# Second feed-forward of a two-stage block in fp32: order of GpSimd's subtractions, place of the sums' split, waits per bank, and x folded by two additions

## The chip, the core and the metric

The kernel runs on one core of a Trainium2 chip. The metric is the device time in microseconds (us) of one execution. A core has TensorE (matrix multiplications into eight PSUM banks of 128 x 512 fp32), VectorE, ScalarE, GpSimd, and SyncE, which here only issues transfers. Each engine works through its own list of instructions in order, and the engines wait for each other by semaphores. In the profile they are PE (PEld is TensorE's loading of weights), DVE, ACT, POOL and SP.

## The reference

The input is x, 2048 rows of 1024. Two stages follow each other, each with a residual addition and a normalisation over the row:

```
s  = silu(x @ w_gate.T);  s[the half of each row with the smallest |s|] = 0
x1 = layernorm(x + (s * (x @ w_up.T)) @ w_down.T)           # 2752 hidden

lin(x, wq, A, B) = x @ tile(wq, (1, 4)).T + 0.5 * (x @ A.T @ B.T)   # rank 2
y  = layernorm(x1 + lin(silu(lin(x1, w1q, a1, b1)) * lin(x1, w3q, a3, b3), w2q, a2, b2))
```

In the second stage each weight is stored for a quarter of its input width and repeated four times. So x1 may first be folded: its four quarters of 256 columns are added, and the product has a depth of 256 instead of 1024. The same holds for the hidden values, 2752 folded to 688. The low-rank parts use the unfolded values.

## The kernel before

The 2048 rows are four blocks of 512 (`NB`), each four tiles of 128 (`NT`). Products keep fp32 precision by splitting each operand into a high part of the type fp32r and a low part, the rest; `three` (L1357 to L1359) multiplies high by high, high by low and low by high. ScalarE rounds to the high part, GpSimd subtracts to get the low part of weights.

The first stage (gate, up and down products and the search for the median) is not touched. The second stage begins near 1494 us and has these parts:

1. Opening. For each of the eight tiles of blocks 0 and 1 TensorE transposes x1 (`turn_x`, L1511), ScalarE copies the result out of PSUM into one of two buffers `x1T` (L856), TensorE multiplies it by A (`low_rank`, L1528), and VectorE folds it into `xf` (`fold_x`, L1225), rounds (`xsh`) and subtracts (`xsl`). ScalarE may overwrite a buffer when `l_fold` says that the fold two tiles before has read it. After four tiles `low_rank_x` (L1238 to L1241) prepares `lx`, the low-rank part, for TensorE.
2. A pass over the weights, `pairs(0)`, for blocks 0 and 1 (`bb` 0 and 1): 11 steps `p`, each with two blocks. For one step and one block TensorE fills four banks (gate and up of two pieces `i`; the banks alternate between 0 to 3 and 4 to 7), 48 matmuls and 4 small ones (L1566). ScalarE makes `sg` = silu of the gate banks (L879). VectorE multiplies by the up banks (`h`, L1253), adds into `fold` (L1258 to L1262) and accumulates two low-rank sums in `acc` (L1273). After each second step, and after the last, a piece of the folded hidden values is complete: ScalarE rounds it (`hq0h` or `hq1h`, L862) and GpSimd subtracts (`hq0l`, `hq1l`; `low_q`, L628). The weights of a step, w1 and w3, come by two transfers; ScalarE rounds (`w13h`, L846), GpSimd subtracts (`w13l`; `low_13`, through the helper L533). They have two buffers; the transfer for step p + 2 waits until TensorE has used step p for both blocks.
3. `down_2` for blocks 0 and 1, tile by tile: 36 matmuls for the two halves of the output. In between, for tile 0, `low_rank_h` sums `acch` and `accl`, the split of `acc`, over the partitions (L1579, L1580), VectorE makes `t2s` of them (L1296, L1298), and two closing matmuls per tile (L1612) bring in the low-rank part. In between also stand the transposes and low-rank products of the tiles of blocks 2 and 3. VectorE adds the residual (`take_out`, L1308), takes the statistics (L1123, L1125); GpSimd raises the variance to the power of -0.5 (L568); ScalarE scales and sends the tile out (L747).
4. The same pass and `down_2` for blocks 2 and 3.

The order on each engine is written out by hand. On GpSimd step p issues `low_13` for step p + 1, then at the end of a piece `low_q` for block 0 and for block 1 (`pairs`, L631). On VectorE `second(b)` (L1322) is: for odd blocks the split of `acc` (`split_sums`, L1279), then `low_rank_h`, then per tile `fold_x` of block b + 2, with `low_rank_x` at its last tile, `take_out` and `norm_sums`. The first pair of the second pass waits on TensorE for all additions of block 1 (`e_evac` at 16), since they read banks 0 to 3.

Of the kernel before, what the change touches and what calls it, by code (L numbers as in the profile page):

```python
# [17 lines left out]
F32 = mybir.dt.float32  # L18
# [7 lines left out]
P = 128  # L26
# [31 lines left out]
Q4 = 4  # L58
# [74 lines left out]
def ends(p):  # L133

    return p % 2 == 1 or p == PAIRS - 1
# [38 lines left out]
def program(nc, xT, xtok, wg, wu, wd, w13, w2, a13, a2, b1, b3, b2, out):  # L174
    x1 = nc.dram_tensor("x1", (NB, P, NT, H), F32, kind="Internal").ap()
    with ExitStack() as ctx:
# [11 lines left out]
        def sb(name, shape, dt, size, offset=None):  # L188
            n = size
            for d in shape[1:]:  # L190
                n *= d
            o = at["next"] if offset is None else offset
            if offset is None:
                at["next"] = -(-(o + n) // 32) * 32
                assert at["next"] <= start + room, (name, at["next"] - start)
            at[name] = o
            return nc.alloc_sbuf_tensor_at(name, shape, dt, offset=o)
# [112 lines left out]
        rest = put("rest", [P, TB], F32)  # L310
        sel = put("sel", [P, R, LR], F32R)
        assert over["at"] <= at["mags"]
        b2raw = sb("b2raw", [P, H], F32, 4, offset=at["t2s"])

        def down_done(name, h):
# [205 lines left out]
        def _(pool):  # L521
# [103 lines left out]
            def low_q(h, c, bb):  # L625
                rows = rows_of(c)
                pool.wait_ge(qh_done, FOLDS * h + 2 * c + bb + 1)
                nc.gpsimd.tensor_tensor(hql[bb][0:rows, c, :], fold[bb][0:rows, c, :], hqh[bb][0:rows, c, :].bitcast(F32),  # L628
                                        ALU.subtract).then_inc(ql_done, 1)

            def pairs(h):  # L631
                for p in range(PAIRS):
                    if p < PAIRS - 1:
                        low_13(h, p + 1)
                    if h == 0 and p == 3:
                        inv_std(NB - 1)
                    for bb in range(2):
                        if ends(p):
                            low_q(h, p // 2, bb)

            low_13(0, 0)
            pairs(0)
# [282 lines left out]
        def _(dve):  # L925
# [192 lines left out]
            def norm_sums(n, tile, tiles=range(NT), whole=slice(0, NT)):  # L1118


                for t in tiles:
                    for i in range(2):
                        step(V.bn_stats(stats[:, t, i, :], tile(t)[:, i * 512:(i + 1) * 512]))  # L1123
                    st.done_apart(passed_dve)
                    step(V.bn_aggr(mv[:, t, :], stats[:, t, :, :].rearrange("p n s -> p (n s)")))  # L1125
                if tiles[-1] == whole.stop - 1:
                    st.done()
                    if n:
                        dve.wait_ge(norm_done, NT * min(n, 2 * NB - 1))
                        dve.sem_inc(passed_dve, 1)  # L1130
                    V.tensor_scalar(ve[:, whole], mv[:, whole, 1], EPS, None, ALU.add).then_inc(ve_ready, 1)
# [86 lines left out]
            def fold_x(b, t):  # L1218

                i = NT * b + t  # L1220
                dve.wait_ge(x1t_ready, 2 * (i + 1))
                if b >= 2 and t == 0:
                    dve.wait_ge(uu_done, 4 * PAIRS)
                st.done()
                V.tensor_reduce(xf[:], x1T[:, i % 2, :, :].rearrange("p (q h) t -> p h t q", q=Q4), AX.X, ALU.add)\  # L1225
                    .then_inc(l_fold, 1)
                dve.wait_ge(l_fold, i + 1)
                tt = slice(t * P, (t + 1) * P)
                step(V.tensor_copy(xsh[:, b % 2, :, tt], xf[:]))
                st.done()  # L1230
                step(V.tensor_tensor(xsl[:, b % 2, :, tt], xf[:], xsh[:, b % 2, :, tt].bitcast(F32), ALU.subtract))

            def low_rank_x(b):

                dve.wait_ge(t1_done, NT * (b + 1))
                bank, x = banks[(1, 5, 7, 7)[b]], lx[0:LX, b % 2, :]
                st.done()
                step(V.tensor_copy(x, bank[0:LX, :]))  # L1238
                step(V.tensor_scalar(rest[0:LX, :], bank[0:LX, :], split_x[0:LX, 0:1], None, ALU.mult))
                st.done()  # L1240
                step(V.scalar_tensor_tensor(out=x, in0=x.bitcast(F32), scalar=split_x[0:LX, 1:2],  # L1241
                                            in1=rest[0:LX, :], op0=ALU.mult, op1=ALU.add))
                st.done()
                dve.sem_inc(l_ready, 1)
# [34 lines left out]
            def split_sums(b):  # L1279

                if b:
                    dve.wait_ge(t2_done, b)
                st.done()
                step(V.tensor_copy(acch[:, :, :], acc[:, b % 2, :, :]))
                st.done()
                V.tensor_tensor(accl[:, b % 2, :, :], acc[:, b % 2, :, :], acch[:, :, :].bitcast(F32), ALU.subtract)\  # L1286
                    .then_inc(acc_ready, 1)
                dve.wait_ge(acc_ready, b + 1)
# [12 lines left out]
            def take_out(b, t):  # L1301

                if t == 0:
                    dve.wait_ge(y_in[b % 2], (32, 16)[b % 2] * (b // 2 + 1))
                for n in range(2):
                    dve.wait_ge(e_done, 2 * NT * b + 2 * t + n + 1)
                    s = y_tile(b, t)[:, n * 512:(n + 1) * 512]
                    V.tensor_tensor(s, banks[2 * (t % 2) + n][:, :], s, ALU.add).then_inc(e_evac, 1)  # L1308
# [12 lines left out]

            def second(b):  # L1322

                if b % 2:
                    split_sums(b)
                low_rank_h(b)
                last = b == NB - 1
                for t in range(NT):
                    if b + 2 < NB:
                        fold_x(b + 2, t)  # L1330
                        if t == NT - 1:
                            low_rank_x(b + 2)
                    take_out(b, t)
                    dve.wait_ge(e_evac, 2 * NT * b + 2 * (t + 1))
                    n = NB + b + (last and t == NT - 1)
                    norm_sums(n, lambda t: y_tile(b, t), [t], slice(0, NT) if not last else FRONT if t < NT - 1 else BACK)
                    if last and t == NT - 2:
                        norm_bias(n, FRONT)
                norm_bias(NB + b + last, BACK if last else slice(0, NT))
# [12 lines left out]
        def _(pe):  # L1352
# [179 lines left out]
            def pair(h, p, bb):  # L1532

                s, c, rows, n = number(h, p, bb), p // 2, rows_of(p // 2), PAIRS * h + p
                if bb == 0:
                    pe.wait_ge(w13_lo, 2 * n + 2)
                    pe.sem_inc(passed_pe, 1)
                if p == 0:
                    pe.wait_ge(l_ready, 2 * h + bb + 1)
                    pe.sem_inc(passed_pe, 1)  # L1540
                    if h == 0:
                        pe.wait_ge(d_evac, 8 * NB)
                        pe.wait_ge(x1t_ready, 4 * NT)
                    else:
                        pe.wait_ge((e_evac, t2_ready)[bb], (4 * NT, 2)[bb])
                        pe.wait_ge(x1t_ready, 8 * NT)
                    pe.sem_inc(passed_pe, 1)
                xh, xl = xsh[:, bb, :, :], xsl[:, bb, :, :]
                for i in range(2):
                    for w in range(2):  # L1550
                        dst = banks[4 * (s % 2) + 2 * i + w][0:rows, :]
                        if p:
                            pe.wait_ge((s_done, h_done)[w], 2 * (s - 2) + i + 1)
                            pe.sem_inc(passed_pe, 1)
                        for k in range(KQ):
                            mm = slice(k * 256 + i * P, k * 256 + i * P + rows)
                            ins = three(dst, w13h[:, n % 2, w, mm], w13l[:, n % 2, w, mm], xh[:, k, :], xl[:, k, :],
                                        k == 0, False)
                if bb == 1:
                    ins.then_inc(w13_used, 1)  # L1560
                for i in range(2):
                    mm = slice((2 * p + i) * P, (2 * p + i) * P + rows) if p < PAIRS - 1 else \
                        slice(2 * p * P + i * rows, 2 * p * P + (i + 1) * rows)
                    for w, done in enumerate((gg_done, uu_done)):
                        p0 = QUAD[2 * i + w]
                        nc.tensor.matmul(banks[4 * (s % 2) + 2 * i + w][0:rows, :], b13[p0:p0 + 3 * R, mm],  # L1566
                                         lx[p0:p0 + 3 * R, bb, :], start=False, stop=True).then_inc(done, 1)
# [139 lines left out]
```

## Time and profile before

Three runs took 1990.75, 1989.9 and 1989.43 us, a median of 1989.9. The profiled execution took 1995.52 us, and its span is 1993.7 us.

| | |
|---|---|
| TensorE busy | 1945.2 us (98% of the span) |
| VectorE, ScalarE, GpSimd busy | 1239.1, 730.9, 921.6 us |
| opening, 1492 to 1529 us: TensorE, VectorE busy | 32.91, 33.59 us |
| first pass, 1529 to 1667: TensorE, VectorE, GpSimd | 130.59, 130.38, 46.39 us |
| blocks 0 and 1 down, 1667 to 1770: TensorE, VectorE | 95.38, 60.24 us |
| second pass, 1770 to 1909: TensorE, VectorE, GpSimd | 136.28, 126.30, 44.85 us |
| blocks 2 and 3 down, 1909 to 1994: TensorE, VectorE | 73.85, 35.65 us |
| one split of the sums (L1284, L1286) | 0.70 and 1.24 us |

The stages are read from the timelines: where the opening's last low-rank product, the passes' last small matmuls and the closing matmuls stand. Matmuls are pipelined, so TensorE's busy time contains overlap; a stop is read from the idle time in front of a row and from the distance of two starts.

### The profile page before, as it was taken

The numbers are of one execution on the slowest core, as the hardware profiler recorded it, in microseconds if no ns is written. First come the engines' busy times: TensorE is split into PE (matmuls) and PEld (weight loads), VectorE is DVE, ScalarE is ACT, GpSimd is POOL, SyncE is SP. The second block draws the span as 40 slices with busy tenths as digits, with TensorE's granted clock in tenths as the row PEclk, the third lists the DMA queues.
The fourth block names the chain that finished last, engine by engine and source line by source line (L and its number), as shares of the span: only waits on it lengthen the run. The fifth ranks groups of instructions, "written<-read, shape, count | busy, mean of one in ns | idle before, by whom it ended". The sixth has DMA issues, their size and how long they took to land. (4 is left out here: it accounts for less than half of the span.)

```text
span 1993.7 us, 24714 instructions
## 1 busy us (share of the span) xinstructions
PE 1945.2 (98%) x9312; PEld 1607.8 (81%) x9312; DVE 1239.1 (62%) x1809; ACT 730.9 (37%) x1196; POOL 921.6 (46%) x722
## 2 busy tenths in 40 slices
PE   8999999999999999999999999999999999999997
PEld 6887878888888888888888888887887677777776
DVE  0147975689764237986523589762028998569963
ACT  4346434472333336423243462322233331113311
POOL 6446884346546444554464445544481341013310
PEclk9999999999999999999999999999999999999999
DMA  4333333224434332434333333435332131201212
GB/s 137 99 92 94 105 114 90 86 90 141 129 95 127 96 95 90 138 100 132 95 122 97 92 132 99 136 90 170 135 101 75 64 124 67 84 32 69 101 43 85
DMA packets 96994, 202.62 MB, mean 102 GB/s; under 512 B 10980, under 2 KB 15076, under 8 KB 95568
## 3 DMA queue, kind: packets, MB, share of 16 engines
q1 hardware_dynamic: 92264, 184.23, 29.7%
q10 hardware_dynamic: 4608, 16.78, 2.1%
q8 instruction: 74, 1.21, 0.3%
q14 instruction: 48, 0.39, 0.1%
HBM read 184.19 MB, written 16.78 MB: 101 GB/s over the span
## 5 line engine op out<-in xcount | busy, mean ns | idle before, releaser
L533 POOL TENSOR_TENSOR wl<-w_in_place,wh 128x512 fp32r<-128x512 f32 (+2 forms) x528 | 712.8, 1353 | 660.9 <-ACT wh L659 660.6
L659 ACT CAST wh<-w_in_place 128x512 fp32r<-128x512 f32 (+2 forms) x528 | 322.3, 612 | 770.5 <-DMA w_in_place<-in_wu 285.2
L1357 PE MATMUL bank<-wh,xTh 128*128 128x512 f32 (+1 forms) x1536 | 571.9, 372 | 12.2 <-POOL wl L533 12.2
L1359 PE MATMUL bank<-wh,xTl 128*128 128x512 f32 (+1 forms) x1536 | 569.4, 371 | 0.0
L1358 PE MATMUL bank<-wl,xTh 128*128 128x512 f32 (+1 forms) x1536 | 569.2, 371 | 0.0
L1357 PEld LDWEIGHTS bank<-wh,xTh 128*128 128x128 f32 x1536 | 290.1, 189 | 63.7 <-issue 7.8
L1359 PEld LDWEIGHTS bank<-wh,xTl 128*128 128x128 f32 x1536 | 290.0, 189 | 50.5
L1358 PEld LDWEIGHTS bank<-wl,xTh 128*128 128x128 f32 x1536 | 290.2, 189 | 49.4
L1357 PE MATMUL bank<-wh,hTh 128*128 128x512 f32 (+1 forms) x704 | 275.0, 391 | 3.0 <-POOL wl L533 2.8
L1358 PE MATMUL bank<-wl,hTh 128*128 128x512 f32 (+1 forms) x704 | 274.7, 390 | 0.0
L1359 PE MATMUL bank<-wh,hTl 128*128 128x512 f32 (+1 forms) x704 | 274.4, 390 | 0.0
L952 DVE TENSOR_SCALAR sgn<-v 128x512 int8<-128x512 f32 (+1 forms) x72 | 51.6, 716 | 182.9 <-ACT v L685 182.9
L708 ACT ACTIVATE junka<-v,negt 128x1376 int8<-128x1376 f32 x96 | 138.3, 1441 | 71.4 <-DVE negt L960 71.4
L1357 PEld LDWEIGHTS bank<-wh,hTh 128*128 128x128 f32 (+1 forms) x704 | 132.5, 188 | 31.3 <-POOL wl L533 3.2
L1357 PE MATMUL bank<-xsh,w13h 128*128 128x512 f32 (+1 forms) x352 | 143.6, 408 | 13.8 <-POOL w13l L533 8.6
L1359 PEld LDWEIGHTS bank<-wh,hTl 128*128 128x128 f32 (+1 forms) x704 | 132.6, 188 | 27.7
L1358 PEld LDWEIGHTS bank<-wl,hTh 128*128 128x128 f32 (+1 forms) x704 | 132.6, 188 | 27.4
L1273 DVE SCALAR_TENSOR_TENSOR acc<-h,a2raw,acc 128x512 f32<-128x512 f32 (+1 forms) x168 | 151.2, 941 | 1.6
L966 DVE TENSOR_SCALAR_CACHE_REDUCE junkd<-v,tc 128x2752 int8<-128x2752 f32 x48 | 147.7, 3076 | 0.9
L1358 PE MATMUL bank<-xsl,w13h 128*128 128x512 f32 (+1 forms) x352 | 138.8, 394 | 0.0
L1359 PE MATMUL bank<-xsh,w13l 128*128 128x512 f32 (+1 forms) x352 | 138.5, 394 | 0.0
L533 POOL TENSOR_TENSOR w13l<-w_in_place,w13h 128x512 fp32r<-128x512 f32 x44 | 67.7, 1560 | 119.5 <-ACT w13h L846 119.5
(138 smaller groups left out, 2148.3 us busy)
## 6 DMA issues: line engine op xcount, KB each, us to landing
w_in_place<-in_wg SPq DMA_DIRECT2D x160, 256.0 KB, 2.6
w_in_place<-in_wu SPq DMA_DIRECT2D x160, 256.0 KB, 2.6
w_in_place<-in_wd SPq DMA_DIRECT2D x160, 256.0 KB, 2.6
w_in_place<-in_w SPq DMA_DIRECT2D x54, 256.0 KB, 2.9
x_in_place<-in_xT SPq DMA_DIRECT2D x32, 256.0 KB, 3.7
y<-in_xtok SPq DMA_DIRECT2D x4, 2048.0 KB, 8.6
x<-y ACTq DMA_DIRECT2D x16, 512.0 KB, 4.1
xa<-x SPq DMA_DIRECT2D x16, 512.0 KB, 4.0
```

The costliest lines, as they stand in the source:

```text
L533: nc.gpsimd.tensor_tensor(lo, landed, hi.bitcast(F32), ALU.subtract).then_inc(done, 1)
L659: nc.scalar.copy(hi, piece).then_inc(hi_done, 1)
L708: ins = nc.scalar.activation(junka[:, :], v[:, t, h * (I // 2):(h + 1) * (I // 2)], ACT.Sign, bias=negt[:, t:t + 1], accum_out=ssum[:, t - ...
L952: step(V.tensor_scalar(sgn[:, t, cols(j)], s, 0.0, 2.0, ALU.is_ge, ALU.mult))
L966: step(V.tensor_scalar(junkd[:, :], v[:, t, :], tc[:, 0, t:t + 1], None, ALU.is_lt, ALU.add, accum_out=tc[:, 1, t:t + 1]))
L1273: step(V.scalar_tensor_tensor(out=part, in0=h2[0:rows, i, :], scalar=w, in1=part, op0=ALU.mult, op1=ALU.add))
L1357: nc.tensor.matmul(dst, ah, bh, start=start, stop=False)
L1358: nc.tensor.matmul(dst, ah, bl, start=False, stop=False)
L1359: return nc.tensor.matmul(dst, al, bh, start=False, stop=stop)
```

## The change

On GpSimd the low part for block 1 (`low_q(.., 1)`) is issued one step later, behind the weights' subtractions of that step. VectorE splits the sums of block 1 (and 3) after tile 1 of block 0 (and 2). The addition of the residual now stands ahead of `low_rank_x`. TensorE's first pair of the second pass waits for each bank's own addition. x is folded by two additions, with a buffer `halves` that lies where `rest` lies; `l_fold` is raised after the first.

```diff
+        halves = sb("halves", [P, KH // 2, P], F32, 4, offset=at["rest"])
...
-                    for bb in range(2):
-                        if ends(p):
-                            low_q(h, p // 2, bb)
+                    if p and ends(p - 1):
+                        low_q(h, (p - 1) // 2, 1)
+                    if ends(p):
+                        low_q(h, p // 2, 0)
+                low_q(h, CQ - 1, 1)
...
-                V.tensor_reduce(xf[:], x1T[:, i % 2, :, :].rearrange("p (q h) t -> p h t q", q=Q4), AX.X, ALU.add)\
-                    .then_inc(l_fold, 1)
+                V.tensor_tensor(halves[:], x1T[:, i % 2, 0:KH // 2, :], x1T[:, i % 2, KH // 2:KH, :], ALU.add).then_inc(l_fold, 1)
                 dve.wait_ge(l_fold, i + 1)
+                step(V.tensor_tensor(xf[:], halves[:, 0:KQ, :], halves[:, KQ:2 * KQ, :], ALU.add))
+                st.done()
...
-                if b % 2:
-                    split_sums(b)
                 low_rank_h(b)
                 last = b == NB - 1
                 for t in range(NT):
                     if b + 2 < NB:
                         fold_x(b + 2, t)
-                        if t == NT - 1:
-                            low_rank_x(b + 2)
                     take_out(b, t)
+                    if b + 2 < NB and t == NT - 1:
+                        low_rank_x(b + 2)
                     dve.wait_ge(e_evac, 2 * NT * b + 2 * (t + 1))
                     n = NB + b + (last and t == NT - 1)
                     norm_sums(n, lambda t: y_tile(b, t), [t], slice(0, NT) if not last else FRONT if t < NT - 1 else BACK)
+                    if b % 2 == 0 and t == 1:
+                        split_sums(b + 1)
...
                     else:
-                        pe.wait_ge((e_evac, t2_ready)[bb], (4 * NT, 2)[bb])
                         pe.wait_ge(x1t_ready, 8 * NT)
+                        if bb:
+                            pe.wait_ge(t2_ready, 2)
...
                             pe.wait_ge((s_done, h_done)[w], 2 * (s - 2) + i + 1)
                             pe.sem_inc(passed_pe, 1)
+                        elif h and not bb:
+                            pe.wait_ge(e_evac, 4 * NT - 3 + 2 * i + w)
+                            pe.sem_inc(passed_pe, 1)
```

## Rows read from the trace of the kernel before

**Rows 1.** The page, part 1: busy time, share of the span, instructions.
```profile
PE 1945.2 (98%) x9312; PEld 1607.8 (81%) x9312; DVE 1239.1 (62%) x1809; ACT 730.9 (37%) x1196; POOL 921.6 (46%) x722
```

**Rows 2.** TensorE's waits, 1500 to 1994: waiter, awaited, total us, times, longest.
```profile
PE bank L1357 <- POOL w13l L533: 8.6, 8, 2.5
PE bank L1579 <- DVE accl L1286: 6.9, 2, 4.5
```

**Rows 3.** Timeline around both waits for `accl`: start, us, engine, instruction [idle before].
```profile
1717.77 0.39 PE L1359 MATMUL bank<-w2h,hq1l 112*128 112x512 f32 x1
...
1722.64 0.71 PE L1579 MATMUL bank<-acch,sel 128*96 128x512 f32 x1 [4.48 <-DVE accl L1286]
...
1952.11 0.70 PE L1579 MATMUL bank<-acch,sel 128*96 128x512 f32 x1 [2.46 <-DVE accl L1286]
```

**Rows 4.** Windows behind three stops: PE, PEld, DVE, ACT, POOL busy, clock, DMA.
```profile
1722.50:1727.00 4.50, 4.36 (x15) 3.60 (x16) 1.37 (x2) 0.62 (x2) 0.00 (x0) 0.52 0.00 0
1770.30:1775.00 4.70, 4.64 (x13) 3.72 (x14) 2.85 (x5) 0.00 (x0) 2.68 (x3) 0.64 0.00 0
1952.00:1956.50 4.50, 4.39 (x12) 3.34 (x13) 1.37 (x2) 3.35 (x3) 0.00 (x0) 0.62 0.82 334
```

**Rows 5.** Timeline, end of block 1 and start of the second pass.
```profile
1766.36 0.71 PE L1612 MATMUL bank<-b2s,t2s 96*128 96x512 f32 x2
...
1768.92 1.29 DVE L1308 TENSOR_TENSOR y<-bank,y 128x512 f32<-128x512 f32 x2
...
1770.36 0.47 PE L1357 MATMUL bank<-xsh,w13h 128*128 128x512 f32 x1 [3.29 <-DVE y L1308]
```

**Rows 6.** Timeline of the opening.
```profile
1517.09 1.94 DVE L1225 TENSOR_REDUCE xf<-x1T 128x256 f32<-128x1024 f32 x1
...
1519.40 0.42 DVE L1231 TENSOR_TENSOR xsl<-xf,xsh 128x256 fp32r<-128x256 f32 x1
...
1520.37 1.96 PE L1528 MATMUL bank<-x1T,a13s 128*102 128x128 f32 x16 [0.87 <-ACT x1T L856]
...
1529.18 0.47 PE L1357 MATMUL bank<-xsh,w13h 128*128 128x512 f32 x1 [0.93 <-DVEq L1244]
```

**Rows 7.** VectorE by form, 1529 to 1667, last row 1777 to 1909.
```profile
L1273 DVE SCALAR_TENSOR_TENSOR acc<-h,a2raw,acc 128x512 f32<-128x512 f32 x76 | 71.2, 977 | 0.7
L1253 DVE TENSOR_TENSOR h<-bank,sg 128x512 f32<-128x512 f32 x40 | 25.8, 686 | 4.9 <-ACT sg L879 3.0 <-DVE acc L1273 1.1
L1258 DVE TENSOR_TENSOR fold<-h 128x512 f32<-128x512 f32 x10 | 7.0, 701 | 0.3
...
L1273 DVE SCALAR_TENSOR_TENSOR acc<-h,a2raw,acc 128x512 f32<-128x512 f32 x76 | 66.9, 921 | 0.7
```

**Rows 8.** Timeline, four accumulations with GpSimd idle.
```profile
1648.30 2.85 DVE L1273 SCALAR_TENSOR_TENSOR acc<-h,a2raw,acc 128x512 f32<-128x512 f32 x4
```

**Rows 9.** GpSimd's `w13l`, 1529 to 1667: ns minimum/median/maximum, first and last start.
```profile
L533 POOL TENSOR_TENSOR w13l<-w_in_place,w13h x18: 1279/1728/1812, 1538.3 to 1644.0; 128x512 fp32r<-128x512 f32 x18
```

**Rows 10.** Timeline of one order on GpSimd in the first pass.
```profile
1630.24 0.62 ACT L846 CAST w13h<-w_in_place 128x512 fp32r<-128x512 f32 x1 [0.33 <-DMA w_in_place<-in_w]
...
1633.24 1.09 ACT L879 ACTIVATE sg<-bank 128x512 f32<-128x512 f32 x2 [2.38 <-PE bank L1566]
...
1635.37 1.74 POOL L628 TENSOR_TENSOR hq1l<-fold,hq1h 128x512 fp32r<-128x512 f32 x1 [4.87 <-ACT hq1h L862]
...
1637.08 3.41 POOL L533 TENSOR_TENSOR w13l<-w_in_place,w13h 128x512 fp32r<-128x512 f32 x2
...
1639.55 1.29 DVE L1253 TENSOR_TENSOR h<-bank,sg 128x512 f32<-128x512 f32 x2 [0.19 <-DVE acc L1273]
```

**Rows 11.** Timeline, `t2s` and the closing matmuls, blocks 0 and 2.
```profile
1676.11 0.68 DVE L1298 TENSOR_TENSOR t2s<-bank,t2s 32x512 fp32r<-32x512 f32 x1
...
1679.21 0.71 PE L1612 MATMUL bank<-b2s,t2s 96*128 96x512 f32 x2
...
1918.77 0.70 PE L1612 MATMUL bank<-b2s,t2s 96*128 96x512 f32 x2 [0.15 <-DVE t2s L1298]
```

## The prediction

> **What bounds the kernel now.** I read the page first: TensorE is busy 98% of the span [rows 1]. So the question is only where it stands still, and the change touches nothing before the second feed-forward, about 1494 to 1994 us. The table of waits for that stretch gives TensorE's stops by cause: 8.6 us in 8 stops for the low weight halves `w13l` from GpSimd and 6.9 us in 2 for `accl` from VectorE [rows 2]; a single one of 3.3 us waits for a residual addition on VectorE [rows 5]. The timelines then show each stop from the last start before it to the first start after it; TensorE's matmuls start 0.23 us apart at full clock, and the modelled length of a matmul hides 0.17 us of each stop. Last I looked at VectorE's groups by form, because it is what TensorE waits for once GpSimd is not: in the 138 us of the first pass over the weights, all but some 8 us of its time is work, and the 4.9 us before `h` are the main gap [rows 7].
>
> **Sums split earlier (`split_sums` of blocks 1 and 3).** TensorE started its last block-1 matmul before the stop at 1717.77 and went on at 1722.64 [rows 3]: 4.87 less one pitch, 4.64 us. The second stop shows 2.46 + 0.17 = 2.63 us. Behind both the granted clock fell to the 1.2 GHz level for some matmuls: it was 0.52 over 4.5 us and 0.62 over 4.5 us, so 2.16 and 1.71 us of full-speed time were lost [rows 4]. VectorE now splits after tile 1 of the block before, where it sits idle between tiles: in blocks 0 and 1 a tile takes TensorE 11.4 us and VectorE about 6, in blocks 2 and 3 8.7 and 3. The 1.94 us moved there (0.7 + 1.24) are hidden; without that cover they would cost 1.94 each. Late next is `t2s` for the closing matmuls of tile 0: TensorE reaches them at 1717.9 + 0.9 (sums) + 0.9 (transposes) + 4.1 (18 matmuls) + 1.75 (low rank) = 1725.5. VectorE ends normalising at about 1721.1 and makes `t2s` in 1.4, 1722.6. No new stop. `low_rank_x(2)` now stands behind the addition of the last tile; it ends near 1717.6 and is asked for at 1723.8. Nothing is late behind it. Sum: 4.64 + 2.16 + 2.63 + 1.71 = 11.1 us.
>
> **Waits per bank, `take_out` before `low_rank_x`.** The last closing matmuls of block 1 start at 1766.36; the first of the second pass starts at 1770.36, because VectorE added the residual only from 1768.92, behind the split of x's low-rank part [rows 5]. 4.00 less 0.44 for the two matmuls is 3.56 us, and the clock behind it was 0.64 over 4.7 us: 1.69 more [rows 4]. After the change the addition runs from about 1767.0 to 1768.3, banks 0 and 1 wait for tile 2's additions (long done), and bank 2 is first written 12 matmuls, 2.7 us, after the start near 1766.8, at 1769.5. The next pair needs `lx` at 1773.1 and VectorE has it at about 1770.5; the order on VectorE (addition, `lx`, statistics) has idle time behind it (4.3 us before the first `h` of the pass). Four waits and increments more: under 0.1 us in all. Sum: 5.2 us.
>
> **x folded by two additions.** The reduction took 1.94 us [rows 6]; an addition of 128x512 takes 0.70 [rows 7], a subtraction of 128x256 0.42 [rows 6], and there is a short wait between: a tile's fold goes from 2.84 us to about 2.0, and the buffer of x is given back after 0.7 rather than 1.94. That is on the path in the opening only (tiles 0 to 7), where ScalarE's copy waits for the buffer and TensorE for ScalarE: stops of 0.88 and 0.87 us before 1517.53 and 1520.37 and of 0.93 before 1529.18, where the second pair waits for VectorE's chain [rows 6], which show the second and the third. From starts: 1.03, 1.08 and 0.99. With the buffer 1.2 us earlier ScalarE's copies of tiles 6 and 7 end near 1515.0 and 1517.7, and TensorE asks for them at 1516.4 and 1518.2. `lx` of block 1 ends near 1524.1, asked for at 1526.0. All three go: 3.1 us. In the later stages the folds lie in VectorE's idle time and bring nothing.
>
> In words of the Trainium skill (SBUF — State Buffer, Who interferes with whom) a reduction never contends with GpSimd on this chip, while a VectorE instruction with two SBUF inputs and a GpSimd instruction that reads SBUF lock each other out for a whole instruction. The rows agree on the additions (below). By that rule the two additions of tile 7, which meet GpSimd's two subtractions of 1520.8, would lose up to 2.6 us against a margin of 1.9, and this item would be 2.4 instead of 3.1.
>
> **Other order on GpSimd.** Before, `hq1l` (1635.37) goes ahead of the two `w13l` subtractions (1637.08 to 1640.49), though the high halves were ready by 1630.9 [rows 10]. After, these run from about 1630.5, and the end of the pair at 1639.2 is not held up: all 8 stops of 8.6 us (10 from starts) lose their cause. But VectorE sets the next limit. It has two sets of four banks, so it may run some 6 us late before TensorE waits for `h`; in the first pass it already is 5.6 us late: `sg` starts at 1633.24 and `h` at 1639.55 [rows 10], 6.3 us, where a free VectorE starts 0.7 us after `sg`; and from 1541 to 1677 it has no idle time beyond signals. So what TensorE gains in the first pass is what VectorE leaves at its end: `t2s` is ready at 1676.8 and the closing matmuls start at 1679.21 without having waited [rows 11]. Of these 2.4 us I take 2.0, since `acc_ready` (1669.5, wanted at 1671.4) leaves 1.9. In the second pass the closing matmuls already waited for `t2s` until 1918.77 [rows 11], so TensorE's 2.6 us there bring only what VectorE's own chain shortens. It was 0.4 us late at its last pair but one and had 0.5 us idle near 1879; with stops gone it starts each pair earlier and ends about 1.0 earlier. Sum 3.0 us.
>
> This holds if GpSimd disturbs VectorE as much as now. An accumulation `acc` takes 2.85 for four undisturbed, 0.71 each [rows 8], but on average 71.2/76 = 0.94 in the first pass and 66.9/76 = 0.88 in the second [rows 7]: 17 and 13 us, and folds in the second 3 more. GpSimd's subtractions, some 30 a pass, take 1.28 undisturbed and 1.73 in the middle [rows 9]. None lost would give the passes 17 and 16 us of VectorE time, more than the stops; all 30 met at 1.28 would be 38, so 21 more each. In the new order of four pairs I lay out, with VectorE 2 us late: `hq0l` half met, the first `w13l` beside `h` (which reads a bank), the second met, `hq1l` met, of the next two one met: 3.5 of 6, where now 4 are. I take no change. The bounds for this item are 11.5 gained (all stops, with 1.7 of clock at 1641) and 8 lost.
>
> **Sum.** 11.1 + 5.2 + 3.1 + 3.0 = 22.4 us. The profiled execution took 1995.5 us (span 1993.7 and 1.8 around it), so it would be 1973.1; the median of the runs is 5.6 lower, 1989.9, and gives 1967.5.
>
> **Rivals.**
> (a) GpSimd's locks grow. In the second pass ten `hq` subtractions now lie beside `h`; moved, each meets an accumulation and costs about 1.05: 10.5, less the 3 of slack, and the last item is 4.5 lost: 1975. For it: `hq1l` moves from right behind the split to later work; against: the first pass has them exposed already and is no slower by more than 1 us. The Trainium skill's rule of the exclusive lock (same section) is this mechanism; the rows' 0.94 against 0.71 agree with it.
> (b) VectorE is no limit, since the locks fall beside `h`: every GpSimd stop comes back, 11.5 instead of 3.0: 1959. Against: VectorE's lateness of 5.6.
> (c) A split or `t2s` is late all the same, or the clock falls at another stop: one of the early stops stays, 3 to 4.6 us: 1971.5.
> (d) The other side: all subtractions meet two-input work in both passes. 43 us more on VectorE, less 5 of slack, against 19.4 gained: 2008. It is slower than before once some 24 of the 43 come, four of five subtractions met. Against: a quarter of VectorE's time is `h`, and it lies there by chance at least.
> (e) The change moves waits without effect because TensorE is limited elsewhere: no. The stops are on the chain itself.
>
> **Chances.** Forecast 0.65 (its own range 1964 to 1971), (a) 0.15, (b) 0.08, (c) 0.08, (d) 0.03, (e) 0.01. The range of 1962.5 to 1974.5 leaves out (b), (d) and half of (a). What can be told from no change is 0.2%, 4 us: faster 0.96, same 0.01, slower 0.03.
>
> **What would show it.** No stop by `accl` near 1712 and 1930 and clock 1.0 there; under 0.3 us between the last closing matmul of block 1 and the first of the second pass; opening stops of TensorE only by the transfer `xa`; TensorE's waits in the passes put down to `h` of VectorE, 3 to 7 us, instead of to `w13l`; closing matmuls of blocks 0 and 2 waiting for `t2s`; mean of `acc` within 0.05 of 0.98 and 0.92. Wrong if `acc` is above 1.05, if `w13l` still ends waits, or if the fold's buffer wait stays.

## The result

Five runs of the changed kernel took 1981.2 us in the median (1978.2 to 1982.2), the kernel before 1989.9 (1989.3 to 1993.8). The ratio on record is 0.9944, with a 95% interval of 0.9931 to 0.9957: 11.1 us or 0.56% faster, where the two medians differ by 8.7. In a second session the ratio was 0.9937 (0.9921 to 0.9954). What an edit is worth is given below by its recorded ratio, times the median of the kernel before; the intervals are 2 to 4 us to either side. The forecast was 1967.5, 22.4 us off, with a range from 1962.5 to 1974.5. The direction was right and the size half of what was forecast or less.

The page of the profiled execution (1980.5 us) shows a span 15.0 us shorter than in [rows 1], and the table of TensorE's waits has other causes than [rows 2]. First the page, then the waits from 1490 to 1980 us (waiter, awaited, total, times, longest):

```profile
PE 1942.5 (98%) x9312; PEld 1604.8 (81%) x9312; DVE 1231.4 (62%) x1825; ACT 733.3 (37%) x1196; POOL 922.1 (47%) x722
```
```profile
PE bank L1361 <- DVE h L1257: 6.3, 6, 1.9
PE bank L1620 <- DVE t2s L1302: 1.9, 1, 1.9
PE bank L1515 <- DMA xa<-x: 1.7, 3, 0.9
PE bank L1587 <- DVE accl L1290: 1.2, 2, 0.6
PE bank L1532 <- ACT x1T L859: 0.5, 1, 0.5
```

The 8 stops for `w13l` are gone, and so are the two long ones for `accl`; those left are 0.6 us each and stand at the ends of the passes. Their place is taken by stops for `h` and `t2s` of VectorE. In the timeline of the end of the second pass TensorE, ready at 1892.7, waits for `h`, then for `accl`, then for `t2s`, where before only the 0.15 us of [rows 11] were lost:

```profile
1894.43 0.77 PE L1361 MATMUL bank<-w2h,hq0h 128*128 128x512 f32 x1 [1.73 <-DVE h L1257]
...
1900.91 0.44 PE L1587 MATMUL bank<-acch,sel 128*96 128x512 f32 x1 [0.60 <-DVE accl L1290]
...
1908.03 0.70 PE L1620 MATMUL bank<-b2s,t2s 96*128 96x512 f32 x2 [1.89 <-DVE t2s L1302]
```

The start of the second pass answers to [rows 5]: VectorE adds right behind the closing matmuls and TensorE goes on without a stop, 0.55 us behind them.

```profile
1757.29 0.71 PE L1620 MATMUL bank<-b2s,t2s 96*128 96x512 f32 x2
1757.81 1.29 DVE L1312 TENSOR_TENSOR y<-bank,y 128x512 f32<-128x512 f32 x2 [1.13 <-PE bank L1620]
1757.84 0.40 PE L1361 MATMUL bank<-xsh,w13h 128*128 128x512 f32 x1
```

The windows behind the places of [rows 4] (same columns, the clock third from the end) show 1.00; but behind both stops for `h` it is 0.63, which is part of the time at the 1.2 GHz level (whether that cost time is told at the second trace of this kernel):

```profile
1662.30:1666.80 4.50, 4.44 (x13) 3.57 (x14) 4.33 (x6) 1.07 (x2) 1.73 (x1) 0.63 0.97 402
1894.40:1898.90 4.50, 4.47 (x13) 3.65 (x14) 4.33 (x6) 1.04 (x2) 1.73 (x1) 0.63 0.98 397
1723.00:1727.50 4.50, 4.50 (x23) 3.74 (x22) 2.79 (x5) 0.00 (x0) 0.00 (x0) 1.00 0.15 59
```

To see where the time went I divide every trace at the starts of TensorE's small matmuls (L1566 before) and closing matmuls (L1612 before). "Open" is the time of the first small matmul, "pass" the time from a pass's first small matmul to the first closing matmul behind it, "0-1" the time from the last two closing matmuls of block 0 to the first of block 1, "1-pass 2" and "2-3" likewise behind blocks 1 and 2. The three traces of the kernel before are the one shown in front and two more, taken later.

```
kernel             open     pass 1  0-1    1-pass 2  pass 2  2-3    span
before             1527.7   151.5   19.0   11.2      141.2   13.9   1993.7
before, 2nd trace  1525.6   149.4   18.4   11.2      140.8   13.7   1988.4
before, 3rd trace  1527.0   147.4   19.7    9.7      141.2   12.3   1986.5
changed            1525.6   151.1   12.3    6.1      144.6    9.6   1978.7
changed, 2nd       1525.7   152.5   12.3    6.1      144.6    9.6   1980.2
e1_order_undone    1525.9   150.5   12.3    6.1      141.1    9.6   1974.9
e2_order_alone     1527.2   152.1   19.2   11.3      145.0   13.8   1997.9
e3_no_read         1525.3   140.9   12.3    6.1      138.4    9.6   1961.9
e4_beside_h        1525.2   142.5   12.3    6.1      139.4    9.6   1964.4
e5_beside_h_alone  1526.6   143.4   19.6    9.6      139.4   13.9   1982.0
e6_old_no_read     1524.0   145.4   12.3    6.1      138.4    9.6   1965.0
e7_split_alone     1527.4   149.6   12.3   12.3      141.2    9.6   1981.8
e8_banks_alone     1526.9   147.6   19.3    6.1      141.2   12.3   1982.9
e9_fold_alone      1527.2   146.6   19.9    9.7      141.2   12.3   1986.1
```

Three columns ("0-1", "1-pass 2", "2-3") give what was forecast. The passes do not: the second is 3.4 us longer than before, the first as long as the longest of before.

### The profile page after: what moved, and what is told of

Same layout as the page of the kernel before. It is cut to its first block and busy times, and to the rows that moved or that the text cites. A ratio compares the mean times of both kernels' runs of the same rounds, so it can differ in the third digit from the quotient of the medians.

```text
span 1978.7 us, 24733 instructions
## 1 busy us (share of the span) xinstructions
PE 1942.5 (98%) x9312; PEld 1604.8 (81%) x9312; DVE 1231.4 (62%) x1825; ACT 733.3 (37%) x1196; POOL 922.1 (47%) x722
## 5 line engine op out<-in xcount | busy, mean ns | idle before, releaser
L955 DVE TENSOR_SCALAR sgn<-v 128x512 int8<-128x512 f32 (+1 forms) x72 | 45.9, 638 | 182.3 <-ACT v L688 182.3
L1277 DVE SCALAR_TENSOR_TENSOR acc<-h,a2raw,acc 128x512 f32<-128x512 f32 (+1 forms) x168 | 157.0, 975 | 1.5
```

The source lines that it names most:

```text
L955: step(V.tensor_scalar(sgn[:, t, cols(j)], s, 0.0, 2.0, ALU.is_ge, ALU.mult))
L1277: step(V.scalar_tensor_tensor(out=part, in0=h2[0:rows, i, :], scalar=w, in1=part, op0=ALU.mult, op1=ALU.add))
```

## The experiments

**Theory 1, the locks.** GpSimd's subtractions and VectorE's instructions with two SBUF inputs hold each other up, and the new order moves the `hq` subtractions from beside `h` to beside `fold` and `acc`; VectorE, which ends the passes, gets later. **Rival, the arrival:** the order only lets TensorE arrive earlier at a VectorE that is late anyway, and loses clock there.

**The order undone, and the order alone.**

```diff
-                    if p and ends(p - 1):
-                        low_q(h, (p - 1) // 2, 1)
-                    if ends(p):
-                        low_q(h, p // 2, 0)
-                low_q(h, CQ - 1, 1)
+                    for bb in range(2):
+                        if ends(p):
+                            low_q(h, p // 2, bb)
```

> The changed kernel with GpSimd's old order (low_q of block 0 and 1 together), all else as changed. Theory 1 (locks): the new order makes the hq subtractions meet two-input work on VectorE, which costs the two pass ends about 4 us in the trace (0.6 and 3.5); undone, the time falls from 1981.2 to about 1977, acc in the second pass goes back from 0.952 to about 0.92 us, TensorE again has some 8 stops for w13l. Theory 2 (arrival): the order only lets TensorE arrive earlier at a VectorE that is late anyway, and what is lost is the clock behind the stop at h; undone, the time stays within 1 us of 1981. Theory 3 (the order helps and the baseline was high): undone, it rises by 3 us, to 1984.

Measured: 1972.6 us (1971.2 to 1976.7), ratio to before 0.9897 (0.9879 to 0.9915). TensorE's 8 stops for `w13l` are back, 8.5 us in all, and the kernel is faster with them than without. The mean of `acc` in the second pass is 0.935 us.

> The kernel before with GpSimd's new order alone. Theory 1: slower by about 4 us, 1994, with no w13l stop but stops at h near both pass ends of some 2 us and acc above 0.95 in the second pass. Theory 2: within 1.5 us of 1989.9. Theory 3: faster by 3, 1987.

Measured: 1999.4 us (1996.9 to 2000.2), ratio 1.0037 (1.0024 to 1.0049). Alone the order makes the kernel 7.4 us slower (4.8 to 9.8), and undoing it in the changed one gives 8 to 9 us (8.6 between the medians), about twice what theory 1 had put down. The rival's "within 1.5 us" is out, and so is theory 3 of the expectations, by which the order helps. One sign of theory 1 did not come: `acc` in the second pass is 0.92, not above 0.95; here the 32 additions into `fold` took up more of it, 28.9 us together instead of 26.3. The second pass costs TensorE 141.1 with the old order and 144.6 to 145.0 with the new, with or without the other edits. Why the medians say more than the traces is told below.

What the order does to GpSimd is plain in its own durations. In the second pass of the kernel before, then of the changed one (ns, minimum/median/maximum; the last of the six lies behind the window):

```profile
L628 POOL TENSOR_TENSOR hq1l<-fold,hq1h x5: 1292/1295/1305, 1804.3 to 1904.6; 128x512 fp32r<-128x512 f32 x5
```
```profile
L629 POOL TENSOR_TENSOR hq1l<-fold,hq1h x5: 1498/1740/1742, 1790.1 to 1889.7; 128x512 fp32r<-128x512 f32 x5
```

1.30 us is the undisturbed time, 1.74 that of a subtraction that meets `acc`. Counted over the second pass, 18 of VectorE's 116 instructions on `fold` and `acc` took over 1.15 us in the kernel before and 23 in the changed one, where 0.69 and 0.74 are undisturbed; together they grew by 3.8 us, and the pass by 3.4. Of the 12 `hq` subtractions 2 overlapped such a long instruction before and 11 after; of the `w13l` 16 of 18 before, and 13 of 20 after. The timeline of the changed kernel shows how VectorE falls behind in one step:

```profile
1783.04 1.29 DVE L1257 TENSOR_TENSOR h<-bank,sg 128x512 f32<-128x512 f32 x2 [0.37 <-ACT sg L882]
...
1783.98 1.29 POOL L629 TENSOR_TENSOR hq0l<-fold,hq0h 128x512 fp32r<-128x512 f32 x1 [8.13 <-ACT hq0h L865]
1784.36 1.46 DVE L1264 TENSOR_TENSOR fold<-fold,h 128x512 f32<-128x512 f32 x1
...
1785.31 1.67 POOL L534 TENSOR_TENSOR w13l<-w_in_place,w13h 128x512 fp32r<-128x512 f32 x1
1785.86 1.67 DVE L1266 TENSOR_TENSOR fold<-fold,h 128x512 f32<-128x512 f32 x1
...
1787.43 1.28 POOL L534 TENSOR_TENSOR w13l<-w_in_place,w13h 128x512 fp32r<-128x512 f32 x1 [0.46 <-ACT w13h L849]
1787.45 4.96 DVE L1277 SCALAR_TENSOR_TENSOR acc<-h,a2raw,acc 128x512 f32<-128x512 f32 x4
...
1790.12 1.74 POOL L629 TENSOR_TENSOR hq1l<-fold,hq1h 128x512 fp32r<-128x512 f32 x1 [1.41 <-ACT hq1h L865]
...
1792.60 1.29 DVE L1257 TENSOR_TENSOR h<-bank,sg 128x512 f32<-128x512 f32 x2 [0.19 <-DVE acc L1277]
```

VectorE is idle before 1783.04, so on time. Then two folds take 1.46 and 1.67 us instead of 0.69 and four `acc` 4.96 instead of 2.85 [rows 8]: 3.9 us for one block of one step. `w13l`, which the old order held back behind `hq1l`, now comes right into the folds, and `hq1l` comes into `acc`.

**The reads taken away.** In the changed kernel and in the one with the old order:

```diff
-                nc.gpsimd.tensor_tensor(hql[bb][0:rows, c, :], fold[bb][0:rows, c, :], hqh[bb][0:rows, c, :].bitcast(F32),
-                                        ALU.subtract).then_inc(ql_done, 1)
+                nc.gpsimd.memset(hql[bb][0:rows, c, :].bitcast(F32), 0.0).then_inc(ql_done, 1)
```

> The changed kernel, where GpSimd fills hq0l and hq1l with zeros by a memset instead of subtracting (so the low half of the folded hidden values is left out); same places in the order, but GpSimd reads nothing of SBUF for these 24 instructions. Theory 1: their locks are gone, acc falls below 0.87 in both passes, VectorE is no longer late at the pass ends, the stops of about 2 us at h and t2s go with their clock, about 1971. Theory 2 and 3: the subtractions do not matter to VectorE, 1980 to 1982.

Measured: 1964.3 us (1963.5 to 1965.5), ratio 0.9857 (0.9837 to 0.9878), 17 us below the changed kernel. The stops at the pass ends are gone with their clock (TensorE's waits list only transfers and `x1T`). `acc` fell from 1.00 to 0.81 us in the first pass; in the second only to 0.90, above the 0.87 that was asked for.

> The changed kernel with GpSimd's old order and the hq subtractions replaced by a memset (the low half of the folded hidden values left out). If a subtraction beside h is free, then in the second pass, where the old order put them there, the mean of acc stays within 0.02 of 0.935 and the pass takes 141.1 less at most 1 us; in the first, where VectorE was late and they met acc, it falls below 0.88 and the pass gets 5 us shorter or more. Rival (each GpSimd read costs wherever it lies): acc falls alike in both.

One execution: 1966.9 us. This one did not part the theories as it should. `acc` was 0.94 in the first pass (expected below 0.88) and 0.91 in the second, and the second pass got 2.7 us shorter, not at most 1. The reason in its trace: a memset takes 0.53 us where the subtraction took 1.3, so `w13l`, queued behind it in the old order, is early and its stops of 0.6 us vanish. The edit changed the queue as well as the reads, and so it did in e3: that run is a bound on what the 24 subtractions cost, not the price of the meetings alone.

**The same subtractions, placed beside `h`.** No work is left out here; a semaphore says that `h` is about to start. Of the edit the new lines are shown, and `pairs` as it reads afterwards.

```diff
+                    if i == 0:
+                        dve.sem_inc(h_go, 1)
                     V.tensor_tensor(h2[0:rows, i, :], banks[4 * (s % 2) + 2 * i + 1][0:rows, :], sg[0:rows, i, :], ALU.mult)
...
+            def go(h, p, bb):
+                pool.wait_ge(h_go, number(h, p, bb) + 1)
...
                 for w in range(2):
                     pool.wait_ge(w13_hi, 2 * n + w + 1)
+                    if w and at_h:
+                        go(h, p - 1, 0)
...
+            def pairs(h):
+                low_13(h, 1)
+                for p in range(PAIRS - 2):
+                    low_13(h, p + 2, True)
+                    if h == 0 and p == 2:
+                        inv_std(NB - 1)
+                    if p % 2:
+                        go(h, p + 1, 1)
+                        low_q(h, p // 2, 0)
+                    elif p:
+                        go(h, p + 1, 1)
+                        low_q(h, p // 2 - 1, 1)
+                go(h, PAIRS - 1, 0)
+                low_q(h, CQ - 2, 0)
+                low_q(h, CQ - 2, 1)
+                low_q(h, CQ - 1, 0)
+                low_q(h, CQ - 1, 1)
```

> The changed kernel with a third order on GpSimd: the second subtraction of each w13l and the hq subtractions each wait until VectorE begins the h of a stated pair (a semaphore raised just ahead of h), since h reads a PSUM bank and sg and not two SBUF tiles; four of six subtractions of two steps then lie beside h. One semaphore increment more per pair on VectorE (42, under 0.1 us each). Theory 1: acc below 0.83 in both passes, VectorE on time, TensorE without stops at h, about 1970. Theory 2: no gain, 1981, or slower by up to 3 where a gated w13l is late.

Measured: 1966.7 us (1966.0 to 1967.8), ratio 0.9869 (0.9851 to 0.9887). It beats both kernels. `acc` is 0.76 in the first pass and 0.84 in the second, the latter a little above what was expected (0.83). Long `fold` and `acc` instructions, 23 a pass in the changed kernel, are 9 and 10. The timeline shows a subtraction and `h` together, both in their undisturbed time, then folds of 0.69 and `acc` of 2.86:

```profile
1816.93 1.29 DVE L1272 TENSOR_TENSOR h<-bank,sg 128x512 f32<-128x512 f32 x2 [0.31 <-ACT sg L895]
1816.99 1.30 POOL L535 TENSOR_TENSOR w13l<-w_in_place,w13h 128x512 fp32r<-128x512 f32 x1 [2.37 <-DVEq L1271]
1818.26 0.69 DVE L1279 TENSOR_TENSOR fold<-fold,h 128x512 f32<-128x512 f32 x1
1818.98 0.69 DVE L1281 TENSOR_TENSOR fold<-fold,h 128x512 f32<-128x512 f32 x1
1819.59 2.86 DVE L1292 SCALAR_TENSOR_TENSOR acc<-h,a2raw,acc 128x512 f32<-128x512 f32 x4
```

In the second pass VectorE has 9.7 us of idle time before its 40 `h` of full height (3.7 in the changed kernel). In the first it is still up to 4.4 us late, but no stop of TensorE is put down to `h` or `acc` in either pass, and TensorE runs both at granted clock 1.00. The instructions of GpSimd are the same in number and kind as in the changed kernel. Their places differ, VectorE raises one semaphore more per pair, and the kernel is 14.5 us faster (1981.2 less 1966.7).

> The kernel before with only the third order on GpSimd (subtractions beside h). Theory 1 (locks): the passes lose what they lose in the version with all edits, 9.0 us in the first and 1.8 in the second against the kernel before, about 1981; all stops for w13l gone while those for accl and the residual stay. Rival (the gain needs the other edits, since only they make TensorE early): 1988 or more.

Measured: 1983.5 us (1983.1 to 1984.3), ratio 0.9953 (0.9938 to 0.9969), 9.4 us off, with passes of 143.4 and 139.4. The stops for `w13l` are down to one of 0.4 us. The rival is out: the placement pays without the other edits.

**The kernel before again.**

> The kernel before, unchanged, for another trace: its runs lie between 1986 and 2000. Theory A (stops of the passes): the two passes over the weights differ between executions, since the w13l stops hang on transfers and locks; first small matmul of a pass to the closing matmuls of its first block, 151.5 and 141.2 us in the trace at hand, varies by 2 us or more. Theory B (first stage): the passes take the same within 0.5 us and the second stage starts earlier or later than 1494.

> As the run before it, one more execution of the kernel before. Theory A: the stretches of the two passes vary by 2 us or more among the three traces. Theory B: they agree within 0.5 us and the start of the second stage varies by several.

1990.2 and 1988.4 us. The first pass took 151.5, 149.4 and 147.4 us in three executions of one program, the second pass the same within 0.4: theory A holds for the first pass alone. The first small matmul also comes earlier or later, by 2.2. VectorE's lateness tells why. Lateness is the start of `h` less the start of the small matmuls and the 1.26 us that a free VectorE takes; here for pairs 11 to 22 of the first pass, and for the second pass of the changed kernel:

```
before, pass 1             3.6 4.2 5.7 6.4 3.6 4.1 5.6 6.3 2.0 1.5 1.1 1.8
before, 2nd trace, pass 1  2.0 1.6 1.2 1.8 1.8 1.4 0.9 1.8 1.7 1.3 0.8 1.5
before, 3rd trace, pass 1  2.0 1.6 1.2 1.8 1.8 1.4 0.9 1.8 1.7 1.3 0.9 1.6
before, pass 2             1.6 1.2 0.8 1.6 1.3 0.9 0.8 1.6 1.2 0.9 0.4 1.5
changed, pass 1            3.7 5.3 5.7 6.5 5.2 6.2 6.6 7.1 5.3 5.1 5.5 7.1
changed, pass 2            2.5 3.1 4.7 4.5 3.2 4.7 5.2 6.0 4.7 5.1 5.6 7.2
e4_beside_h, pass 2        0.1 0.1 0.8 0.1 0.1 0.1 0.8 0.1 0.1 0.2 0.1 2.0
```

The traces show the old order running in two ways. About 1 to 2 us late, VectorE stays so, and few of the 12 `hq` subtractions of a pass meet a long `fold` or `acc`: 2 in the second pass, 4 in the first of the two later traces, which were in this way for its latter half. About 4 to 6 late, it stays so up to the 18th pair in one trace, and 8 of 12 do. The execution shown in front was in the second way for most of its first pass; the two others left it after ten pairs. These two differ before: at the sixth pair the second trace is 8.8 us late and the third 6.7, and in the second TensorE waits 2.1 us for `h`. What decides between the ways is open. TensorE's waits hang on it too: the kernel before stood 8 times and 8.6 us for `w13l` in the first trace [rows 2], 5 times and 4.8 to 4.9 us in the two others. The profiled execution of e1_order_undone, the slowest of its five, was in the second way for 18 pairs as well. It fits this that the order's price is 3.8 to 4.2 us between first traces and 7.4 to 9 us between the sets of runs. The new order is in the second way in all three of its traces, and in the second pass as well. The clock behind the old stops is a second source of spread. In the third trace it did not fall behind the residual stop, which was as long as before:

```profile
1717.80:1722.30 4.50, 4.39 (x15) 3.57 (x16) 1.37 (x2) 0.65 (x2) 0.00 (x0) 0.50 0.00 0
1766.30:1771.00 4.70, 4.68 (x21) 3.88 (x22) 2.81 (x5) 0.00 (x0) 2.73 (x3) 1.00 0.00 0
1946.50:1951.00 4.50, 4.47 (x20) 3.64 (x21) 1.37 (x2) 3.28 (x3) 0.00 (x0) 1.00 0.84 341
```

**The other three edits, each alone** (their parts of the diff in front on the kernel before), and the changed kernel again.

> The kernel before with only the earlier split of the sums. If the item stands as forecast, the stretch from the last closing matmul of block 0 to the first of block 1 falls from 18.4 to 19.7 us to 12.3 and that from block 2 to 3 from 12.3 to 13.9 to 9.6: 9 to 11 us off, 0.45 to 0.55%. Rival (the next wait, for t2s, takes it over): half of that or less.

Measured: 1982.1 us, ratio 0.9944 (0.9928 to 0.9961), 11.2 us off. The two stretches are 12.3 and 9.6, as expected.

> The kernel before with only the waits per bank and take_out ahead of low_rank_x. As forecast: last closing matmul of block 1 to the first small matmul of the second pass 6.1 us instead of 9.7 (clock kept) or 11.2 (clock lost): 3.5 to 5.1 us off. Rival (VectorE starts the second pass late instead and gives it back by the pass's end): the second pass gets longer by as much.

Measured: 1987.4 us, ratio 0.9974 (0.9963 to 0.9984), 5.2 us off. The stretch is 6.1 and the second pass stays at 141.2.

> The kernel before with only the fold by two additions. As forecast: the two stops for x1T and the one for VectorE's queue in the opening go, 3.1 us off. Rival (the additions meet GpSimd's reads, which the reduction did not): under 2 off.

Measured: 1989.5 us, ratio 0.9987 (0.9975 to 0.9999), 2.6 us off. The two later stops for `x1T` and the one for VectorE's queue are gone; one for the transfer `xa` stands at 0.25. The rival's "under 2" lies inside the interval.

> The changed kernel once more, for a second trace of it and for a median on the chip of these runs. If the new order holds VectorE in one regime, its stretches of the two passes agree with the first trace within 0.5 us (151.1 and 144.6), unlike those of the kernel before (147.4 to 151.5 in the first pass). Rival: they vary as much.

Measured: 1980.3 us (1978.9 to 1982.0), ratio 0.9937 (0.9921 to 0.9954). The second pass is 144.6 again; the first is 152.5, 1.4 more than in the first trace and outside the 0.5 that was expected, though VectorE's lateness agrees within 0.1 us at all but a few pairs. VectorE runs in one way, and the 1.4 us are TensorE's clock. These are windows of the second trace behind the stop for `h`, behind the one for `accl`, and behind `h` in the second pass, then the first pass's stop for `accl` in the first trace and in the second:

```profile
1662.30:1666.80 4.50, 4.38 (x18) 3.30 (x18) 4.33 (x6) 1.14 (x2) 1.75 (x1) 1.00 0.98 404
1668.90:1673.40 4.50, 4.47 (x17) 3.67 (x18) 4.43 (x6) 1.43 (x3) 1.74 (x1) 0.62 0.02 5
1895.80:1900.30 4.50, 4.34 (x18) 3.30 (x18) 4.33 (x6) 1.07 (x2) 1.74 (x1) 1.00 1.00 408
```
```profile
1668.85 0.45 PE L1587 MATMUL bank<-acch,sel 128*96 128x512 f32 x1 [0.60 <-DVE accl L1290]
```
```profile
1668.93 0.69 PE L1587 MATMUL bank<-acch,sel 128*96 128x512 f32 x1 [2.13 <-DVE accl L1290]
```

With the clock kept behind `h` TensorE only waits longer for `accl`, 2.13 us instead of 0.60, and goes on at the same time. So the 1.7 us of clock behind `h` cost nothing. In the first pass of this execution the clock fell behind `accl` instead, where TensorE waits for nothing more until its closing matmuls, and these came at 1678.20 instead of 1676.72.

## Why the forecast failed

**Split earlier: right.** 11.1 us forecast, 11.2 measured alone (7.8 to 14.3, and in its trace the stretch "1-pass 2" grew by 1.1); the stretches 0-1 and 2-3 fell by 6.7 and 4.3 against the same execution of before. No wait for `t2s` took over.

**Waits per bank: right.** 5.2 forecast, 5.2 measured (3.2 to 7.4). Of these 1.7 were clock, and the clock does not fall in each execution; against the third trace the stretch fell by 3.6. That forecast and measurement agree to a tenth here, and for the split, is in part luck.

**Fold: right within its error.** 3.1 forecast, 2.6 measured alone (0.2 to 5.0 by the interval). All three stops went, but the transfer `xa`, twice 0.37 us late in the changed trace, was not in the sum. The additions do meet GpSimd's reads: one in the opening took 1.57 and one 1.38 instead of 0.69 and 0.42, and the rounding behind the latter 1.27 instead of 0.29; TensorE did not wait for any of them.

**Other order on GpSimd: wrong, and all of the miss.** Forecast 3.0 gained. Measured 7.4 lost alone and 8 to 9 in company (0.9944 and 0.9937 against 0.9897). The three right items give 19.0 and the order takes 7.4 of it, 11.6 left; measured were 11.1 and 12.5. The step that failed is "In the new order of four pairs I lay out, with VectorE 2 us late: ... 3.5 of 6, where now 4 are. I take no change." The lateness was assumed where it had to be followed. In the changed second pass VectorE is on time at the fourth pair and 3.4 late at the fifth, since `hq0l`, both `w13l` and `hq1l` all meet folds or `acc`; from there it stays at 1.6 to 7.2. So the gain of 1.0 at the end of the second pass was a loss of 3.4, by trace. In the first pass "what VectorE leaves at its end", 2.0, was read from an execution that was itself in the late way; against the two others the pass got longer by 1.7 to 5.1. Rival (a) had the mechanism and, for the profiled execution, the size (4.5 lost, 3.8 and 4.2 by trace). It counted ten `hq` subtractions of the second pass as free before and met after; 10 of 12 were free before and 1 after. It left out that fewer `w13l` are then met, which gave part of it back. Its reason against itself, that the first pass "has them exposed already and is no slower by more than 1 us", was true of that one execution only. The sign that was to show a miss was blind as well: `acc` at 1.00 and 0.95 stayed within 0.05 of 0.98 and 0.92. On the 84 `acc` of a pass 0.05 us are 4.2, more than the 3.4 that the second pass lost.

**The base.** The sum was taken from a profile 5.6 us above its median and the difference carried over. For the three right items this did no harm. For the order it did: the profiled first pass, 151.5 us where the two others took 149.4 and 147.4, had already paid 2 to 4 us of what the new order makes permanent. And 3.7 of the 8.6 us of `w13l` stops on which the item was built stood in that execution only.

**The stop at `h` behind the passes.** The forecast named 3 to 7 us of waits for `h` and was right in that (6.3), but gave them no price. The stops at the pass ends were followed by 1.7 us of lost clock each in the first trace and by none in the second, and the second pass took 144.6 both times: its loss is VectorE's lateness alone. In the first pass too TensorE started the sums at the same time with and without that loss.

## What to carry to other kernels

When an order is changed so that one engine stops waiting, follow the engine that is next for a full cycle, from the lateness it really has, and see which of its instructions the moved ones will meet; a total of collisions "as now" is no estimate. And a sign that is to show a miss needs an allowance smaller than the miss: count it on all the instructions of the group. Two engines that hold each other up can have two lasting ways of running: compare the lateness in two or three executions before trusting one. The remedy here was no freer order but a stricter one: a wait that starts GpSimd's subtraction with the one VectorE instruction that does not read two SBUF tiles.

## What the runs showed of the hardware

- A GpSimd subtraction of 128x512 beside `h` (inputs PSUM and SBUF) takes 1.29 to 1.30 us and leaves `h` at 0.69: over both passes no `h` of any trace took less than 0.67 or more than 0.69. Beside `acc` or `fold` (two SBUF inputs) one of the two waits: the subtraction takes up to 1.74, or the VectorE instruction about 1 us more. A memset of the same tile by GpSimd took 0.53. The Trainium skill (SBUF — State Buffer, Who interferes with whom) speaks of a lock held for a whole instruction; the doubled and tripled durations of single additions (1.57, 1.38) agree.
- Stops of the same length in the same place were followed by a fall of TensorE's clock in one execution (0.64 behind the 3.29 us stop of [rows 5], 0.63 behind the 1.73 us stop for `h`) and not in another (1.00 behind both).
- The kernel before spread over about 8.5 us in each of three sessions (1986.2 to 1994.6 in 15 runs, with a sixteenth of 2000.5 whose mean clock was 0.943; 1987.4 to 1995.9 in 9; 1987.8 to 1996.2 in 17). With the subtractions beside `h` it spread over 1.2 in 5 runs although the long stops and their clock were left (e5_beside_h_alone), and over 3.3 in 11 with the new order (e2_order_alone), which fits two ways of running as the main source.
